# A one-core decoder block: q and k projected token-major and turned by transposing DMAs, instead of projected channel-major and scaled by a broadcast

## The chip, the cores and the metric

The kernel runs on one core of one Trainium2 chip. The metric is the device time of one execution in microseconds (us), lower is better. The kernel before takes 1475.8 us (median of three runs, 1473.98 to 1477.23).

## What is computed

A decoder block on `x` of 16 batches x 256 tokens x 512 channels: an attention with quantised weights and activations, then a mixing stage (a long convolution per head group), then a gated feed-forward. Only the first part is touched by the change:

```python
def _L0_attn_ref(x, w_qkv, w_proj):        # x: layer-normed, (16, 256, 512)
    def _bitlinear(x, w):                  # activations rounded per token, weights to {-1, 0, 1}
        xq, wq = act_quant(x), weight_quant(w)
        return jnp.einsum('bnc,oc->bno', xq, wq)
    qkv = _bitlinear(x, w_qkv).reshape(B, N, 3, H, D)      # 16 heads of 32 channels
    q, k, v = qkv[:, :, 0], qkv[:, :, 1], qkv[:, :, 2]
    attn = jnp.einsum('bnhd,bmhd->bhnm', q, k) * SCALE
    attn = softmax(where(causal, attn, NEG))
    out = jnp.einsum('bhnm,bmhd->bnhd', attn, v).reshape(B, N, C)
    return _bitlinear(out, w_proj)
```

`act_quant` rounds each token's 512 values to integers in steps of c, a number per token (its largest magnitude / 127). The kernel multiplies the integers and multiplies the products by c afterwards.

## The kernel before

Five engine programs are written out by hand with semaphores between them; each engine runs its own list in order (PE the matmuls, DVE, ACT, POOL the element-wise work, SP the DMAs). The attention part is a software pipeline over steps t. A step serves one **pair** of heads; a batch has 8 pairs, so a batch takes 8 steps, and what a batch needs once (norm, projections, finishing) hangs on fixed steps of those eight. Work of about four batches is in flight: batch b+4 is normed and projected while the scores of a later pair and the finishing of batch b run.

In each step, in the order of each engine's list:
- PE: `weigh` (probabilities x v, L686/L687), `row_max` (scores for the row maxima into `s_qk`, L629 to L634), `probabilities` (scores again, transposed, into `s_kq`, L659 to L669), then the once-per-batch work: `project_out` (L702), `multiply_v` (L616), `turn_xq` (L596), `spread_c` (L587), `turn_max` (L640), `turn_oq` (L694), `multiply_qk` (L607). `row_max` of a pair waits for DVE's `take_max` of the pair before it.
- ACT: `weighed` (L1502), `exponentials` (pT, L1488), `high_part` (pH, L1494), finishing of a batch (L1511 is its step size, of one output row), `high_qk` (L1474), norm and rounding, copies.
- DVE: `take_max` (blockmax, L1014), `scale_qk` (L994), v's halves (L1004, L1007), norm statistics, finishing (o_sb L1059, L1065, L1068, x_sb L1077).
- POOL: `low_part` (pL, L1846), `low_qk` (L1839), sums and pieces of feed-forward weights.
- SP: per batch one `x_scratch` store, 16 `pack` DMAs (L2057), one load of x, one store and one load of a weight piece.

Where q and k come from, for one batch (four parts of 128 x 512 each, one PSUM bank each, over four steps):
1. `multiply_qk` writes a bank **channel-major** (channels on partitions, tokens along the free axis), 8 matmuls of 256 columns.
2. The token's scale c then varies along the free axis, so it must be a row on all partitions: ACT writes it on a diagonal (`diagonal`, L1428), PE multiplies it by ones (`spread_c`, L587), ACT copies that to `cbc` (`copy_c`, L1435).
3. DVE multiplies the bank by `cbc` into `qkt`, f32 (`scale_qk`, L994); this frees the bank.
4. ACT copies `qkt` to f16, the high half (`high_qk`, L1474); POOL subtracts, the low half (`low_qk`, L1839; for batch 0 two of the four on DVE, L984).
5. SP regroups high and low halves with 16 DMAs into `pack` (`pack_qk`), which `row_max` and `probabilities` read.

The three PSUM banks of `misc1` go round among all once-per-batch users; a user waits for the release of the use three before.

These lines place the work (project step k of batch b is t = 8b - 13 + k):

```python
# PE: k = 0..3 multiply_qk(b, k)
# DVE:  if 1 <= k < 5: scale_qk(b, k - 1)
# ACT:  if 2 <= k < 6: high_qk(b, k - 2)        (after exponentials, high_part, finish)
# POOL: if 3 <= k < 7: low_qk(b, k - 3)
# SP:   if k == 7: pack_qk(b)
```

Batches 0 and 1 are prepared ahead of the steps.

## Time and profile before

| | |
|---|---|
| median of three runs | 1475.8 us (1473.98 to 1477.23) |
| the profiled execution | 1472.95 us, of which the span is 1471.2 us |
| mean granted PE clock | 0.99 of full speed |
| busy, share of the span | PE 95%, DVE 85%, POOL 79%, ACT 59% |
| attention part | about 26 to 470 us of the span |
| mixing and feed-forward | from about 470 us to the end; the change does not touch them |

Busy time says how long an engine had something in it; a matmul's bar is longer than the time it holds the engine, since matmuls are pipelined. The same holds in small for ACT and DVE: the bars of neighbours overlap by some 0.1 us, so what an instruction costs its engine is the distance from its start to the next one's start. A waiting engine is told by what ended its wait; the chain of waits follows the work that ended last backwards.

### The profile page before, as it was taken

The page shows a single profiled execution, that of the slowest core. Times are in us where ns is not written, and L with a number is a line of the kernel's source. Part 1 is how long each engine was busy: PE and PEld are TensorE (multiplying, and loading weights), DVE is VectorE, ACT ScalarE, POOL GpSimd, SP SyncE. Part 2 cuts the span into 40 slices and gives each one's busy share as a digit, 9 for nine tenths or more (in the row PEclk, how much of TensorE's full clock was granted, in tenths as well). Part 3 has the DMA queues.
Part 4 walks back from the last instruction along what each step waited for, and adds up shares of the span by engine and source line. Part 5 has one row for each costly group of instructions (what it writes and reads, how often), then busy time and mean ns, then how long its engine had stood idle before and what let it go on. Part 6 is the DMA issues. An engine that isn't in the chain of part 4 may idle for free.

```text
span 1471.2 us, 24208 instructions
## 1 busy us (share of the span) xinstructions
PE 1391.6 (95%) x8529; PEld 776.5 (53%) x8529; DVE 1243.6 (85%) x1987; ACT 870.4 (59%) x1434; POOL 1165.6 (79%) x893
## 2 busy tenths in 40 slices
PE   3788999999987997999999999999999999999998
PEld 2577878888765443344444444444444444444443
DVE  6889999999988897998888898899899889888521
ACT  5689999999876223555454545455465456544341
POOL 3389999999982878988887888878877887888432
PEclk9899999999999999999999999999999999999999
DMA  5554656565523533223423422432333333240001
GB/s 193 147 130 122 167 142 164 144 158 137 142 70 99 175 84 79 65 53 62 101 44 72 101 51 51 93 76 47 79 68 76 65 72 64 63 97 15 23 15 29
DMA packets 171588, 133.59 MB, mean 91 GB/s; under 512 B 120500, under 2 KB 124748, under 8 KB 171468
## 3 DMA queue, kind: packets, MB, share of 16 engines
q1 hardware_dynamic: 171276, 131.91, 36.5%
q8 instruction: 68, 1.11, 0.3%
q14 instruction: 52, 0.43, 0.1%
q10 hardware_dynamic: 192, 0.14, 0.1%
HBM read 50.67 MB, written 19.92 MB: 48 GB/s over the span
## 4 chain that ended last, share of the span: by engine, by line
PE 64%; DVE 13%; POOL 8%; issue 7%; ACT 6%; DMA 1%; SPq 0%; POOLq 0%; DVEq 0%; ACTq 0%
PE gu L868 20%; PE gu L882 11%; PE shared_bank L813 9%; PE y L837 3%; PE y L832 3%; PE y L829 3%; PE y L835 3%; PE y L838 3%; POOL pL L1846 2%; DVE blockmax L1014 2%; DVE o_sb L1059 2%; DVE z L1277 1%; DVE qkt L994 1%; PE misc L702 1%; ACT pH L1494 1%
## 5 line engine op out<-in xcount | busy, mean ns | idle before, releaser
L1718 ACT ACTIVATE shared<-shared_bank 128x512 f32<-128x512 f32 x162 | 96.2, 594 | 319.5 <-PE shared_bank L813 319.5
L1274 DVE TENSOR_TENSOR y<-shared,y 128x512 f32<-128x512 f32 x324 | 224.1, 692 | 42.1 <-ACT shared L1718 22.9
L1846 POOL TENSOR_TENSOR pL<-pT,pH 128x768 f16<-128x768 f32 x119 | 200.6, 1687 | 14.0 <-ACT pH L1494 7.8
L1281 DVE TENSOR_REDUCE oT<-z 128x64 f32<-128x512 f32 x256 | 175.6, 686 | 8.7
L868 PE MATMUL gu<-fT,wg 128*128 128x512 f16 x768 | 181.4, 379 | 1.5 <-DMA fT<-fnl 1.5
L868 PE MATMUL gu<-fT,wu 128*128 128x512 f16 x768 | 181.4, 379 | 0.0
L1277 DVE TENSOR_TENSOR z<-y,cT 128x512 f32<-128x512 f32 x236 | 162.4, 688 | 10.3 <-PE y L827 4.1
L1982 POOL TENSOR_TENSOR fuL<-fu,fuH 128x512 f16<-128x512 f32 x96 | 111.5, 1162 | 71.0 <-ACT fuH L1733 70.9
L882 PE MATMUL gu<-wd,fuH 128*128 128x512 f16 x384 | 145.5, 379 | 0.0
L882 PE MATMUL gu<-wd,fuL 128*128 128x512 f16 x384 | 145.5, 379 | 0.0
L1918 POOL TENSOR_TENSOR kv<-vT,cT 128x1024 f32<-128x1024 f32 x70 | 137.9, 1971 | 3.1 <-ACT vT L1673 3.1
L868 PEld LDWEIGHTS gu<-fT,wg 128*128 128x128 f16 x768 | 75.1, 98 | 121.0 <-issue 47.9
L868 PEld LDWEIGHTS gu<-fT,wu 128*128 128x128 f16 x768 | 75.1, 98 | 118.2 <-issue 45.7
L1488 ACT ACTIVATE pT<-s_kq,ws 128x768 f32<-128x768 f32 x124 | 111.4, 898 | 25.4 <-PE s_kq L669 19.9
L1014 DVE TENSOR_REDUCE blockmax<-s_qk 128x6 f32<-128x768 f32 x124 | 117.5, 948 | 3.9 <-PE s_qk L634 2.7
L813 PE MATMUL shared_bank<-kv_sum,toep 128*128 128x512 f32 x216 | 110.5, 593 | 0.3 <-POOL kv_sum L1906 0.3
L1906 POOL TENSOR_TENSOR kv_sum<-kv 128x1024 f32<-128x1024 f32 x27 | 63.7, 2360 | 55.0 <-DVE kv L1249 55.0
L1839 POOL TENSOR_TENSOR qkhl<-qkt,qkhl 128x512 f16<-128x512 f32 x62 | 83.9, 1355 | 20.7 <-ACT qkhl L1474 20.7
L1296 DVE SCALAR_TENSOR_TENSOR fu<-gu,cols,sil 128x512 f32<-128x512 f32 x96 | 71.3, 743 | 33.6 <-PE gu L868 33.6
L650 PE MATMUL s_kq<-pack 128*128 128x128 f16 x744 | 96.4, 220 | 0.0
L1494 ACT ACTIVATE pH<-pT 128x768 f16<-128x768 f32 x111 | 93.4, 841 | 0.0
L1249 DVE TENSOR_TENSOR kv<-vT,cT 128x1024 f32<-128x1024 f32 x58 | 74.0, 1276 | 14.2 <-ACT vT L1681 12.4
(251 smaller groups left out, 3589.9 us busy)
## 6 DMA issues: line engine op xcount, KB each, us to landing
pack<-qkhl SPq DMA_DIRECT2D x256, 128.0 KB, 2.6
x_sb<-in_x SPq DMA_DIRECT2D x16, 512.0 KB, 4.3
c_sb<-in_ctx SPq DMA_DIRECT2D x32, 256.0 KB, 4.1
hankel<-in_L_xattn_k SPq DMA_DIRECT2D x32, 256.0 KB, 4.1
out_y<-yo SPq DMA_DIRECT2D x32, 256.0 KB, 2.9
x_grp<-x_scratch SPq DMA_DIRECT2D x30, 256.0 KB, 3.6
x_scratch<-x_sb SPq DMA_DIRECT2D x14, 512.0 KB, 3.0
wraw<-in_L_attn_w_qkv SPq DMA_DIRECT2D x3, 1024.0 KB, 9.8
```

Of the source, the lines that this page charges most:

```text
L813: T.matmul(shared_bank[:], tap(h, (2, 0, 1)[part]), (kv_sum, kv12, kv_sum)[part][:, half * HB:(half + 1) * HB, :, :].rearrange("p b j i -> ...
L868: made = T.matmul(bank[:], (wg, wu)[which][:, cb, ib * P:(ib + 1) * P], fT[:, cb, part, :], start=cb == 0 and part == 0, stop=cb == CB - 1 ...
L882: made = T.matmul(bank[:], src[:, t * P:(t + 1) * P], wd[:, ib, :], start=ib == 0 and part == 0, stop=ib == IB - 1 and part == 1)
L1014: V.tensor_reduce(out=blockmax[b % 2][:, p, :], in_=score_tile(n)[:, 0:6, :], op=ALU.max, axis=AXIS.X, negate=True).then_inc(max_done, 1)
L1274: chain.step(V.tensor_tensor(bank[:], shared[2 * part + half][:], bank[:], op))
L1277: V.tensor_tensor(z[:], y, weight, ALU.mult).then_inc(m_zm, 1)
L1281: V.tensor_reduce(out=oT[h % 2][:, lb, own].rearrange("p (b j) -> p b j", b=HB), in_=z[:], op=ALU.add, axis=AXIS.X).then_inc(m_z, 1)
L1488: S.activation(pT[n % NP][:], scores_tile(n)[:, 0:6, :], ACT.Exp, scale=ws[:, 4:5]).then_inc(exp_done, 1)
L1494: S.activation(pH[n % NP][:], pT[n % NP][:], ACT.Copy).then_inc(high_act, 1)
L1846: G.tensor_tensor(pL[n % 2][:], pT[n % NP][:], pH[n % NP][:], ALU.subtract).then_inc(low_done, 1)
L1918: G.tensor_tensor(block(h, lb), vT[:, lb, :].rearrange("p (b i) -> p b i", b=B).unsqueeze(2).broadcast_to([P, B, M_POS, M_POS]), cT[h % 2] ...
L1982: G.tensor_tensor(fuL[ib][:], fu[n % 2][:], fuH[:, ib, :], ALU.subtract).then_inc(f_fl, 1)
```

## The change

q and k are projected **token-major** (tokens on partitions), as v already is. Then c is one number per partition, which ACT and DVE can apply while they read the bank: ACT writes the high half (bank x c, f16) straight from PSUM, DVE the low half (bank x c - high) straight from PSUM, both into a new tile `tok`. SP turns each part to channel-major with a transposing DMA (128 tokens x 1024 f16, high and low of one part) into `qkhl`, from where the 16 pack DMAs go on as before. The diagonal, its product with ones, `cbc`, `qkt`, DVE's `scale_qk` and POOL's `low_qk` are gone. ACT's `high_qk` stands one step earlier (k = 1..4) and ahead of `high_part`. A bank is now released by the low half.

(`low_qk` below is in DVE's program, `high_qk` in ACT's, `turn_qk` in SP's.)

```diff
-        qkt = [q(f"qkt{i}", [P, 2, N], F32) for i in range(3)]
+        tok = [q(f"tok{t}", [P, 2, 2, C], F16) for t in range(NT)]
...
-            def spread_c(b):
...
-            def multiply_qk(b, g2):
-                qk, g0 = qk_groups(g2)
-                bank = misc1.take(("qk", b, g2), w, (qk_scaled, 4 * b + g2 + 1))
+            def multiply_qk(b, s):
+                qk, t = token_tile(s)
+                bank = misc1.take(("qk", b, s), w, (qk_low, 4 * b + s + 1))
                 w.wait_ge(xqT_done, 2 * b + 2)
                 wT_ready(w, qk)
-                for g in range(2):
-                    o0 = qk * C + (g0 + g) * P
-                    for cb in range(CB):
-                        made = T.matmul(bank[:, g * N:(g + 1) * N], wqkvT[:, cb, o0:o0 + P], xqT[b % 3][:, cb, :],
-                                        start=cb == 0, stop=cb == CB - 1)
+                for cb in range(CB):
+                    made = T.matmul(bank[:], xqT[b % 3][:, cb, t * P:(t + 1) * P], wqkvT[:, cb, qk * C:(qk + 1) * C],
+                                    start=cb == 0, stop=cb == CB - 1)
...
+            def low_qk(b, s):
+                n, (qk, t) = 4 * b + s, token_tile(s)
+                w.wait_ge(qk_high, n + 1)
+                V.scalar_tensor_tensor(out=tok[t][:, qk, 1, :], in0=misc1.of["qk", b, s][:], scalar=small[b % 4][:, 12 + t:13 + t],
+                                       in1=tok[t][:, qk, 0, :], op0=ALU.mult, op1=ALU.subtract).then_inc(qk_low, 1)
...
                     if 1 <= k < 5:
-                        scale_qk(b, k - 1)
+                        low_qk(b, k - 1)
...
-            def diagonal(b):
...
-            def copy_c(b):
...
+            def high_qk(b, s):
+                n, (qk, t) = 4 * b + s, token_tile(s)
+                w.wait_ge(qk_pe, n + 1)
+                w.wait_ge(c_done, b + 1)
+                if b > 0:
+                    w.wait_ge(qk_turned, 64 * b)
+                S.activation(tok[t][:, qk, 0, :], misc1.of["qk", b, s][:], ACT.Copy, scale=small[b % 4][:, 12 + t:13 + t]).then_inc(qk_high, 1)
...
                 for i, blocks in turning(t - 1):
                     copy_weights(i, blocks)
+                for b, k in project_steps(t):
+                    if 1 <= k < 5:
+                        high_qk(b, k - 1)
                 if (n := pair(t, HIGH)) is not None and high_on_act(n):
                     high_part(n)
...
-                for b, k in project_steps(t):
-                    if 3 <= k < 7:
-                        low_qk(b, k - 3)
...
+            def turn_qk(b, s):
+                qk, t = token_tile(s)
+                w.wait_ge(qk_high, 4 * b + s + 1)
+                w.wait_ge(qk_low, 4 * b + s + 1)
+                if b >= 2:
+                    wait_packed(w, b - 2)
+                Y.dma_start(qkhl[b % 2][:, qk, :, :, t * P:(t + 1) * P].rearrange("p l g n -> p (l g) n"),
+                            tok[t][:, qk].rearrange("p l c -> p (l c)"), transpose=True).then_inc(qk_turned, 16)
...
                 for b, k in project_steps(t):
+                    if 2 <= k < 6:
+                        turn_qk(b, k - 2)
                     if k == 7:
                         pack_qk(b)
```

How the lists move, in the steady part. On **ACT**, in the two steps up to the finishing's step size (L1511 before, L1458 after; `tok` is written by `high_qk`). Before:

```order
L1474 ACTIVATE qkhl<-qkt 128x512
L1419 ACTIVATE xn<-xn,small 128x512
L1502 ACTIVATE oraw<-pv 128x2x130
L1488 ACTIVATE pT<-s_kq,ws 128x768
L1494 ACTIVATE pH<-pT 128x768
L1511 ACTIVATE osmall<-osmall 128x2
L1474 ACTIVATE qkhl<-qkt 128x512
L1428 ACTIVATE diag<-ident,small 128x128 x2
L1502 ACTIVATE oraw<-pv 128x2x130
```

After:

```order
L1421 ACTIVATE tok<-misc,small 128x512
L1441 ACTIVATE pH<-pT 128x768
L1381 ACTIVATE xn<-xn,small 128x512
L1449 ACTIVATE oraw<-pv 128x2x130
L1435 ACTIVATE pT<-s_kq,ws 128x768
L1441 ACTIVATE pH<-pT 128x768
L1458 ACTIVATE osmall<-osmall 128x2
L1449 ACTIVATE oraw<-pv 128x2x130
```

The last of a batch's four high halves stood behind the step size and now stands ahead of it, so all four are ahead of it where three were; the diagonal is gone.

On **SP**, one batch of the steady part. Before:

```order
L2066 DMA x_scratch<-x_sb 128x2x512
L2057 DMA pack<-qkhl 32x2x1024 x16
L2043 DMA x_sb<-in_x 128x2x512
L2082 DMA wq_scratch<-fw_out 128x768
L2077 DMA fw_raw<-in_L_ffn_gate_w 128x768
```

After:

```order
L1996 DMA x_scratch<-x_sb 128x2x512
L1987 DMA pack<-qkhl 32x2x1024 x16
L1975 DMA_TRANSPOSE qkhl<-tok 128x8x128
L1967 DMA x_sb<-in_x 128x2x512
L2012 DMA wq_scratch<-fw_out 128x768
L2007 DMA fw_raw<-in_L_ffn_gate_w 128x768
L1975 DMA_TRANSPOSE qkhl<-tok 128x8x128 x3
```

Four transposes per batch are added, one ahead of the load of x and three behind the weight piece.

## Rows read from the trace of the kernel before

**Rows 1.** Busy time in one batch period: us, then each engine's busy us (instructions).

```profile
219.26:244.08 24.82, 24.64 (x305) 20.20 (x304) 23.32 (x40) 24.29 (x49) 24.63 (x18) 1.00 0.58 152
```

**Rows 2.** Waits in 145 to 370 us: us in total, times, longest.

```profile
DVE small L944 <- ACT small L1403: 5.1, 9, 0.6
...
DVE osmall L1068 <- ACT osmall L1511: 1.8, 9, 0.2
```

**Rows 3.** Chain of waits, one period of it: start us, us, what.

```profile
223.66 0.65 PE misc L587 x4
...
226.35 0.90 ACT pT L1488
...
235.34 0.07 DVE small L944
...
251.16 0.90 ACT pT L1488
```

**Rows 4.** Timeline of ACT in that period: start us, us, instruction.

```profile
230.35 0.84 ACT L1494 ACTIVATE pH<-pT 128x768 f16<-128x768 f32 x1
...
234.08 0.61 ACT L1530 ACTIVATE oqT<-misc 128x512 bf16<-128x512 f32 x1
234.56 0.66 ACT L1474 ACTIVATE qkhl<-qkt 128x512 f16<-128x512 f32 x1
...
240.14 0.61 ACT L1474 ACTIVATE qkhl<-qkt 128x512 f16<-128x512 f32 x1
240.66 0.71 ACT L1419 ACTIVATE xn<-xn,small 128x512 f32<-128x512 f32 x1
241.27 0.36 ACT L1502 ACTIVATE oraw<-pv 128x260 f32<-128x260 f32 x1
```

**Rows 5.** Timeline of DVE in that period; idle time before stands in brackets.

```profile
230.41 0.68 DVE L994 TENSOR_TENSOR qkt<-misc,cbc 128x512 f32<-128x512 f32 x1
...
243.27 0.17 DVE L1068 RECIPROCAL osmall<-osmall 128x2 f32<-128x2 f32 x1 [0.19 <-ACT osmall L1511]
...
248.26 0.95 DVE L1014 TENSOR_REDUCE blockmax<-s_qk 128x6 f32<-128x768 f32 x1
```

**Rows 6.** Timeline of PE there.

```profile
249.53 0.38 PE L629 MATMUL s_qk<-pack 128*128 128x256 f16 x2
```

**Rows 7.** A group of POOL in 120 to 400 us: busy us, mean ns, idle before.

```profile
L1839 POOL TENSOR_TENSOR qkhl<-qkt,qkhl 128x512 f16<-128x512 f32 x46 | 64.1, 1394 | 0.0
```

**Rows 8.** A group of DVE in 120 to 400 us: busy us, mean ns, idle before.

```profile
L1007 DVE SCALAR_TENSOR_TENSOR vHL<-misc,small,vHL 128x512 f16<-128x512 f32 x23 | 17.3, 751 | 0.8
```

**Rows 9.** All instructions of line 1059: ns least/median/most, first and last start.

```profile
L1059 DVE TENSOR_TENSOR o_sb<-oraw,osmall x15: 1221/1524/2602, 111.6 to 451.7; 128x1024 f32<-128x1024 f32 x15
```

**Rows 10.** Transposing DMAs of the mixing part: SP's ns each, then us from issue to landing.

```profile
L2174 SPq DMA_TRANSPOSE c_sb<-planes x30: 1246/1267/1378, 491.0 to 1316.1; - x30
...
DMA to landing us min/median/max: 3.0/3.1/4.9
```

**Rows 11.** Timeline of SP over one batch: its first and last DMA of twenty.

```profile
246.93 0.38 SPq L2066 DMA_DIRECT2D x_scratch<-x_sb  x1
...
259.99 0.43 SPq L2077 DMA_DIRECT2D fw_raw<-in_L_ffn_up_w  x1
```

**Rows 12.** Timeline of batch 0, before the steps.

```profile
26.09 3.65 PE L607 MATMUL misc<-xqT,wqkvT 128*128 128x256 bf16 x32
...
32.09 10.55 SPq L2057 DMA_DIRECT2D pack<-qkhl  x16
...
44.70 0.38 PE L629 MATMUL s_qk<-pack 128*128 128x256 f16 x2 [1.87 <-DMA pack<-qkhl]
...
46.18 0.92 DVE L1014 TENSOR_REDUCE blockmax<-s_qk 128x6 f32<-128x768 f32 x1
```

**Rows 13.** Timeline of ACT in the first full batches.

```profile
100.47 0.90 ACT L1488 ACTIVATE pT<-s_kq,ws 128x768 f32<-128x768 f32 x1 [0.87 <-POOL pL L1846]
...
126.65 0.90 ACT L1488 ACTIVATE pT<-s_kq,ws 128x768 f32<-128x768 f32 x1
```

More of the change, by code:

```diff
@@ L140, in decoder_kernel @@
         xqT = [q(f"xqT{i}", [P, CB, N], BF16) for i in range(3)]
-        diag = q("diag", [P, NT, P], F32)
-        cbc = [q(f"cbc{i}", [P, N], F32) for i in range(2)]
         packs = [q(f"pack{i}", [P, 2, R, GQ, N], F16) for i in range(2)]
@@ L580, in weight_total @@
                 T.matmul(bank[:, 0:n], ones[:], wsums[:, first:first + n], start=True, stop=True).then_inc(wtot_pe, 1)
-            def spread_c(b):
-                bank = misc1.take(("cbc", b), w, (cbc_done, b + 1))
-                w.wait_ge(const_done, C_BASE)
-                w.wait_ge(diag_done, b + 1)
-                for t in range(NT):
-                    made = T.matmul(bank[:, t * P:(t + 1) * P], ones[:], diag[:, t, :], start=True, stop=True)
-                made.then_inc(cbc_pe, 1)
             def turn_xq(b, j):
@@ L1170, in vector_program @@
             for g2 in range(4):
-                scale_qk(0, g2)
-            for g2 in FIRST_LOW_ON_DVE:
-                low_first(g2)
+                low_qk(0, g2)
             max_in(1)
@@ L1419, in round_in @@
                 S.activation(xn[:, t, 0:C], xn[:, t, 0:C], ACT.Copy, bias=ROUND, scale=sm[:, 10 + t:11 + t]).then_inc(xround_done, 1)
-            def diagonal(b):
-                sm = small[b % 4]
-                w.wait_ge(c_done, b + 1)
-                w.wait_ge(const_done, C_BASE)
-                if b > 0:
-                    w.wait_ge(cbc_pe, b)
-                for t in range(NT):
-                    made = S.activation(diag[:, t, :], ident[:], ACT.Copy, scale=sm[:, 12 + t:13 + t])
-                made.then_inc(diag_done, 1)
-            def copy_c(b):
-                w.wait_ge(cbc_pe, b + 1)
-                if b >= 2:
-                    w.wait_ge(qk_scaled, 4 * (b - 1))
-                S.activation(cbc[b % 2][:], misc1.of["cbc", b][:, 0:N], ACT.Copy).then_inc(cbc_done, 1)
             def copy_xqT(b, j):
@@ L1578, in scalar_program @@
             round_weights(0)
-            diagonal(0)
             sign_weights(0)
@@ L1593, in scalar_program @@
                 round_in(1, i)
-            diagonal(1)
             moments(2)
@@ L1626, in scalar_program @@
                             round_in(b, i)
-                    if k == LOAD_AHEAD + 8:
-                        diagonal(b)
                     for j in range(2):
@@ L1868, in gpsimd_program @@
             power_in(1)
-            for g2 in range(4):
-                if g2 not in FIRST_LOW_ON_DVE:
-                    low_qk(0, g2)
             for t in STEPS:
@@ L2104, in sync_program @@
             Y.dma_start(wraw[3][:], w_proj.rearrange("(g t p) c -> g p t c", p=P, t=WB)[0]).then_inc(wraw_in[3], 16)
+            for s in range(4):
+                turn_qk(0, s)
             pack_qk(0)
```

68 lines of the change are left out of this document (9 added, 59 removed).

## The prediction

> **What bounds the kernel now.** I looked first at the busy time of one batch period of the attention part. A period is 24.82 us, and POOL is busy for 24.63 of it, PE 24.64, ACT 24.29, DVE 23.32 [rows 1]. So the shares do not name a bound: four engines are full, and the one that the change relieves most (POOL) looks like the fullest. Two other views are needed. The chain of waits, read over one period, says which loop of waits closes without slack, and the list of waits says which engine waits for which each time round.
>
> The chain does not pass through POOL in the steady part. From the exponential at 226.35 it runs down ACT's list to a small scale, over to DVE at 235.34, down DVE's list, then to PE, and back to ACT's exponential at 251.16 [rows 3]. That is eight steps later, 24.81 us, so this is a loop (**loop A**) that sets the period. Its PE leg holds the spreading of c, 0.65 us [rows 3]. The waits show the hand-overs, nine times in nine batches: DVE waits for ACT's L1403, and, in another place, for ACT's L1511 [rows 2]. The second is a loop of its own (**loop B**): down ACT's list from 226.35 to L1511, which releases DVE at 243.27 [rows 5], 16.92 us; down DVE's list to the blockmax that ends at 248.26 + 0.95 = 249.21 [rows 5], 5.94 us; 0.05 us until PE's `row_max`, which in fact starts at 249.53 [rows 6]; and 251.16 - 249.53 = 1.63 us to the exponential. Sum 24.54, so it has 0.27 us of slack now. Everything in it is order on one engine or a semaphore that the change keeps, so after the change the period cannot be shorter than loop B's new sum.
>
> **What the change does to ACT.** The high half costs 0.52 us of ACT now (240.14 to 240.66 [rows 4]). After, it reads PSUM and takes its scale from a tile. A copy of the same size out of PSUM without such a scale costs 0.48 (234.08 to 234.56 [rows 4]); a copy SBUF to SBUF with one costs 0.61 against the 0.52 without (240.66 to 241.27 [rows 4]), so the scale adds 0.09. I take 0.48 + 0.10 = 0.58, with bounds 0.48 and 0.61. The diagonal and the copy of `cbc` fall away, but ACT does them after L1511 and before 226.35: they lie in neither loop. What lies in them is high halves. They move one step forward. In loop A's ACT leg there is one now and there will be two: 2 x 0.58 - 0.52 = +0.64. In loop B's leg there are three now and all four after: 4 x 0.58 - 3 x 0.52 = +0.76.
>
> **DVE.** Four scalings at 0.68 us [rows 5] become four subtractions of the kind of L1007 at 0.75 [rows 8], +0.07 each, two of them in loop A, none in loop B's DVE leg. A new wait comes with them: DVE's first low half waits for ACT's high half of the same step. ACT would begin it where it now begins pH, 230.35 [rows 4], and end near 231.0; DVE now starts the scaling at 230.41 [rows 5]. DVE's list behind it is late by 0.6 us, `take_max` in it, for which PE's `row_max` waits. As a loop of its own: ACT from 226.35 to 231.0, 4.65; DVE's list from 230.41 to 249.21, 18.80, less its two waits for ACT (5.1 / 9 = 0.57 and 0.19 [rows 2, 5]) and with four times 0.07 more, 18.32; PE 1.68. That is 24.65, below B, so I cost it at nothing; without B's cover it would still be no more than today's period.
>
> **PE.** The 32 matmuls of 256 columns per batch become 16 of 512, the same columns, and I cost that at nothing. The spreading of c leaves loop A, -0.65. In loop B it saves nothing, because there PE is late on DVE's side of the wait.
>
> **Sums.** Loop A: 24.81 + 0.64 + 0.14 - 0.65 = 24.94. Loop B: 24.54 + 0.76 = 25.30. The period goes from 24.81 to 25.30, **+0.49 us**. With the bounds of the high half it is 24.90 or 25.42, so +0.1 to +0.6. L1511 stands behind four high halves in twelve periods (finishing of batches 0 to 11 beside projection of 4 to 15). The first of these is the early stretch below; the other eleven give 11 x 0.49 = **+5.4**.
>
> **POOL.** Its 64 subtractions (62 of them at L1839, mean 1394 ns [rows 7]) go, 5.6 us per batch. In the steady part nobody waits for them. In the first full batches somebody does: ACT's exponential at 100.47 had waited 0.87 us for POOL, and the eight steps to the one at 126.65 took 26.18 us [rows 13]. There loop B is lighter by the two copies of the finished rows (0.48 each [rows 4]), which no batch has yet: 25.30 - 0.96 = 24.34. That saves 1.8, with the wait ahead of it 0.9: **-2.7**, bounds 0 and -4.
>
> **SP and the DMAs.** Four transposes per batch at 1.27 us of SP each, 3.1 us from issue to landing [rows 10]. The twenty DMAs of a batch fill SP from 246.93 to 260.42 [rows 11], 13.5 us; with 5.1 more SP is busy 18.6 of 25. The first transpose comes behind the 16 packs and the others ahead of the store that now waits for x; the last can go once the fourth low half is there, about 243, and lands near 246. Pack starts after that store, at 247.3, as now. The packs land by 261.4 and the scores need them near 269, so 8 us cover this. In **batch 0** nothing covers it. The four parts leave PE 0.9 us apart from 26.09 [rows 12]: part one at 27.0, high half to 27.7, low half to 28.6, then four transposes issued 1.27 apart, the last at about 32.4, landed at 35.5. Pack starts at 32.09 now [rows 12], so it is 3.4 late, and so is the first `row_max`, which waits for the packs (1.87 us at 44.70 [rows 12]). DVE takes that maximum at 46.18, 0.9 later than it could; the delay that DVE's list passes on is about **+2.5**, bounds 1 and 5.
>
> **Total:** 2.5 - 2.7 + 5.4 = +5.2 on the profiled execution, 1472.95, gives 1478.2. The median of the runs, 1475.8, lies 2.85 above that execution, so on it 1481.0. The forecast's own range is 1475 to 1484: 4.4 less to 1.3 more from the high half, some 2 either way from the first batches. A measurement of this kernel can tell about 0.2% (3 us) from no change.
>
> **Rivals.** *1: POOL is the bound, and the kernel gets faster.* For it: POOL is busy 24.63 of 24.82 us [rows 1], and the early stretch shows it as the bound. Against it: in steady state the chain avoids it and nobody waits for it. If loop B is misread (if its hand-overs have slack that a different order opens), PE is next, and it loses the 0.65 of the spreading: 11 x -0.65 = -7.2, with -2.7 and +2.5 it is -7.4, so 1468.4. It decides if the period can reach 24.82 - 0.65 = 24.17: if the high halves in front of L1511 cost 0.3 us each, or if loop B shrinks elsewhere by 1.1. DVE could shrink: o_sb takes 1.22 us at best and 1.52 in the middle, 2.60 at most [rows 9], and the long ones fall together with POOL's work. With 1.22, loop A would be 24.63; loop B's DVE leg does not hold that instruction and stays. The Trainium skill (SBUF — State Buffer, "Who interferes with whom") says that a DVE instruction with two SBUF inputs and a GpSimd instruction that reads SBUF exclude each other for a whole instruction. By that rule the change frees DVE four times a batch, which speaks for this rival; the spread of o_sb agrees with it.
>
> *2: no change that can be told.* The high half costs 0.48 as the plain PSUM copy does; the period is 24.90, so 11 x 0.09 = +1.0 with -2.7 and +2.5 it is +0.8: 1476.6. The same comes if PE or DVE make up part of B.
>
> *3: the transposes become the bound.* SP is full when a transpose holds it for (25.3 - 13.5) / 4 = 2.95 us; alone they take at most 1.38 [rows 10], but none of those stood next to 16 packs. At 3.5 us a batch would take 27.5: +2.2 x 12 = +26, so 1507. That halving the number of q and k matmuls does nothing is part of the forecast, not a rival.
>
> **Chances.** Forecast 0.52, rival 1 0.20, rival 2 0.22, rival 3 0.06. Faster by over 0.2%: rival 1 and the low edge of 2, 0.22. Within 0.2%: most of rival 2 and the low edge of the forecast, 0.25. Slower: the rest, 0.53. The range reaches to rival 1's 1468 and 7 us over the forecast, 1467 to 1488; it leaves out rival 3 and the tails of rival 1.
>
> **What would show it.** Right: the steady period from exponential to exponential is about 25.3; DVE waits for the step size (L1458 after) 0.3 us or more each time; POOL idles 5 us a batch and nobody waits for it; the new high half costs 0.58 from start to start; the first `row_max` stands near 48. Wrong: a period of 24.2 with PE never waiting (rival 1); PE's `row_max` waiting for packs in steady state, or SP without pause (rival 3); DVE waiting long for high halves in each step would mean that ACT is late on PE's qk, which I cost at nothing.

## The result, and the profile after

The changed kernel takes **1481.3 us** (median of 5 runs, 1481.06 to 1482.41); the kernel before took 1473.98 us in the same session (5 runs, 1472.97 to 1477.23). The ratio is **1.0054**, 95% interval 1.0042 to 1.0066: slower, by more than the 0.2% that can be told. Run again later beside other kernels it gave 1.0057 (1.0041 to 1.0074). In one later session two executions, one of each kernel, took about two and two and a half times as long (2950.0 and 3762.11 us); they are left out of every median and ratio here. The forecast of 1481.0 us is met within 0.3, but partly by luck: the forecast difference (+5.2 us) was smaller than the measured one (0.54% of 1474, 8.0 us, interval 6 to 10), and the median that the forecast stood on, 1475.8 of three runs, was 1.8 us above that of the five here, of which those three are the first. On 1473.98 the same sum gives 1479.2. The profiled execution went from 1472.95 to 1481.3 us, +8.35, and that is what has to be accounted for.

I measure by one kind of mark, ACT's exponential of pair 2 of each batch (`pT`, L1435 after, L1488 before), as the prediction did:

| us | before | after | difference |
|---|---|---|---|
| first `row_max` | 44.70 | 49.23 | +4.53 |
| first exponential | 70.30 | 75.19 | +4.89 |
| pair 2, batch 0 to batch 2 | 50.82 | 49.77 | -1.05 |
| steady period, pair 2 to pair 2 | 24.81 | 25.24 | +0.43 |
| last exponential | 454.96 | 460.91 | +5.95 |
| from there to the end of the execution | 1017.99 | 1020.39 | +2.40 |

The steady part answers to [rows 1 to 4]. First the busy times in one period of the changed kernel, columns as in [rows 1]: span, PE, PEld, DVE, ACT, POOL, granted clock, DMA share, GB/s.

```profile
231.40:256.64 25.24, 24.81 (x285) 18.21 (x284) 23.68 (x40) 23.79 (x46) 18.78 (x14) 1.00 0.85 191
```

POOL fell from 24.63 to 18.78 us, as predicted, and the period got longer. ACT's busy time also fell, from 24.29 to 23.79, so once more the shares do not name the bound. The list of waits, 145 to 370 us (total, times, longest):

```profile
POOL pL L1776 <- ACT pH L1441: 37.0, 36, 1.6
POOL pL L1776 <- PE pv L665: 15.0, 9, 1.7
ACT pT L1435 <- PE s_kq L647: 13.1, 27, 0.8
...
DVE tok L958 <- ACT tok L1421: 5.1, 9, 0.6
...
DVE osmall L1032 <- ACT osmall L1458: 3.7, 9, 0.5
```

The wait of DVE for ACT's input step size, first in [rows 2], is gone. The other one, for the finishing step size (L1458, L1511 before), grew from 1.8 to 3.7 us over nine batches, 0.41 us each. The first low half waits 0.57 us each time for its high half, which is new. POOL stands in this list only as the one that waits, most of all for ACT.

The chain of waits of the changed kernel, one period (start, us, what):

```profile
231.40 0.90 ACT pT L1435
...
235.40 0.11 ACT tok L1421
...
247.39 0.78 ACT pT L1435
248.28 0.53 issue
248.81 0.20 ACT osmall L1458
249.11 0.70 DVE stats L902
...
253.99 0.96 DVE blockmax L978
255.00 0.39 PE s_qk L607 x2
...
256.64 0.90 ACT pT L1435
```

This is loop B and no longer loop A [rows 3]: ACT's list from 231.40 without a pause to L1458, then DVE to the blockmax of 253.99, PE, and the exponential 25.24 us after the first one. (The blockmax is DVE's maximum over the scores, for which PE's next scores wait.) ACT's timeline shows what filled the leg:

```profile
235.40 0.69 ACT L1421 ACTIVATE tok<-misc,small 128x512 f16<-128x512 f32 x1
235.97 0.85 ACT L1441 ACTIVATE pH<-pT 128x768 f16<-128x768 f32 x1
...
245.11 0.66 ACT L1421 ACTIVATE tok<-misc,small 128x512 f16<-128x512 f32 x1
245.68 0.83 ACT L1441 ACTIVATE pH<-pT 128x768 f16<-128x768 f32 x1
```

From start to start a high half takes 0.57 us (235.40 to 235.97, 245.11 to 245.68); four of them lie before L1458 (the other two at 238.96 and 241.88). The forecast was 0.58 and four. DVE goes on at 249.03, so ACT's leg is 17.63 us, against a forecast of 16.92 + 0.76 = 17.68.

Batch 0, from the timelines of PE and SP (start, us, instruction, idle before), answers to [rows 12]:

```profile
25.46 5.79 PE L585 MATMUL misc<-wqkvT,xqT 128*128 128x512 bf16 x16 [0.95 <-ACT wqkvT L1413]
...
49.23 0.38 PE L607 MATMUL s_qk<-pack 128*128 128x256 f16 x2 [4.11 <-DMA pack<-qkhl]
```

```profile
28.93 5.69 SPq L1975 DMA_TRANSPOSE qkhl<-tok  x4
36.62 10.42 SPq L1987 DMA_DIRECT2D pack<-qkhl  x16
```

The packs begin 4.53 us later than before (36.62 against 32.09), and the first `row_max` is late by exactly that. The 16 projection matmuls take 5.79 us; the same columns in 32 matmuls took 3.65 [rows 12]. The four transposes hold SP for 5.69 us, and 7.7 us lie between the start of the first and that of the first pack.

### The profile page after: what moved, and what is told of

Read it like the earlier page. It is cut to its first block, busy times and chain, and to the rows that moved or that the text cites. A ratio compares the mean times of both kernels' runs of the same rounds, so it can differ in the third digit from the quotient of the medians.

```text
span 1479.5 us, 23490 instructions
## 1 busy us (share of the span) xinstructions
PE 1392.5 (94%) x8209; PEld 743.1 (50%) x8209; DVE 1245.9 (84%) x1985; ACT 861.0 (58%) x1386; POOL 1079.7 (73%) x831
## 3 DMA queue, kind: packets, MB, share of 16 engines
q8 instruction: 66, 1.08, 0.3%
## 4 chain that ended last, share of the span: by engine, by line
PE 58%; ACT 13%; DVE 12%; issue 7%; POOL 5%; DMA 2%; SPq 1%; POOLq 0%; DVEq 0%; ACTq 0%
PE gu L842 19%; PE gu L856 11%; PE shared_bank L787 8%; ACT pT L1435 3%; ACT pH L1441 3%; PE y L803 3%; PE y L811 3%; PE y L806 3%; PE y L812 3%; PE y L809 3%; DVE blockmax L978 2%; DVE z L1239 2%; ACT oraw L1449 1%; DVE stats L902 1%; DMA v_sb<-planes 1%
## 5 line engine op out<-in xcount | busy, mean ns | idle before, releaser
L1435 ACT ACTIVATE pT<-s_kq,ws 128x768 f32<-128x768 f32 x124 | 111.6, 900 | 34.3 <-PE s_kq L647 33.8
L1672 ACT ACTIVATE fuH<-fu 128x512 f16<-128x512 f32 x96 | 59.7, 621 | 38.4 <-DVE fu L1258 38.4
```

The costliest lines, as they stand in the source:

```text
L1435: S.activation(pT[n % NP][:], scores_tile(n)[:, 0:6, :], ACT.Exp, scale=ws[:, 4:5]).then_inc(exp_done, 1)
```

## The experiments

Twelve runs of kernels, in four sessions, each beside the kernel before on the same chip. "Period" is the steady one from pair 2 to pair 2; "early" is the stretch from batch 0 to batch 2. These and the other columns behind the ratio come from one profiled execution each, so their differences from batch 0 and the mixing part hold scatter: after and after_again are the same kernel.

| kernel | us, median (runs) | ratio to before (95%) | first exp. | early | period | after the last exp. |
|---|---|---|---|---|---|---|
| before (profiled) | | 1 | 70.30 | 50.82 | 24.81 | 1017.99 |
| after (profiled) | 1481.3 (5) | 1.0054 (1.0042-1.0066) | 75.19 | 49.77 | 25.24 | 1020.39 |
| after_again | 1481.87 (5) | 1.0057 (1.0041-1.0074) | 76.66 | 49.76 | 25.23 | 1020.93 |
| step_on_dve | 1479.07 (5) | 1.0048 (1.0035-1.006) | 75.74 | 49.03 | 24.94 | 1020.43 |
| before_step_on_dve | 1474.01 (11) | 1.0012 (1.0003-1.0021) | 70.20 | 51.67 | 24.89 | 1018.64 |
| warm_first | 1481.36 (5) | 1.0062 (1.005-1.0075) | 75.81 | 52.65 | 25.23 | 1020.62 |
| plain_copies | 1479.44 (5) | 1.005 (1.0037-1.0063) | 75.53 | 49.77 | 25.23 | 1020.45 |
| both_steps_on_dve | 1489.38 (5) | 1.0116 (1.0097-1.0134) | 74.77 | 50.06 | 26.06 | 1018.29 |
| before_both_steps_on_dve | 1477.45 (10) | 1.0028 (1.0017-1.0039) | 72.54 | 51.32 | 24.89 | 1021.96 |
| before_no_low_halves | 1468.63 (9) | 0.997 (0.9958-0.9981) | 69.73 | 47.77 | 24.79 | 1019.32 |
| max_before_low | 1477.12 (7) | 1.0028 (1.0018-1.0039) | 73.58 | 48.54 | 24.94 | 1019.73 |
| max_before_low_alone | 1479.04 (5) | 1.0045 (1.0031-1.0058) | 74.85 | 49.23 | 25.23 | 1020.78 |
| single_column_steps | 1480.7 (5) | 1.0059 (1.0047-1.0072) | 75.22 | 49.28 | 25.22 | 1020.23 |
| two_highs_on_pool | 1496.85 (5) | 1.0163 (1.0146-1.018) | 73.80 | 48.48 | 26.79 | 1021.46 |

### Is it loop B? The hand-over taken out

```diff
 # VectorE, finish(b, 3)
+w.wait_ge(omax_done, b + 1)
+V.tensor_scalar(step, am, 1.0 / 127.0, None, ALU.mult).then_inc(ostep_done, 1)
 w.wait_ge(ostep_done, b + 1)
 V.reciprocal(inv, step).then_inc(oscale_done, 1)
 # ScalarE, finish(b, 3)
-w.wait_ge(omax_done, b + 1)
-S.activation(step, am, ACT.Copy, scale=1.0 / 127.0).then_inc(ostep_done, 1)
```

> The changed kernel, with the finishing's step size (largest magnitude / 127) computed by DVE itself in place of ACT's L1458, so that DVE no longer waits there for ACT. Theory (loop B, through four high halves on ACT and that hand-over, sets the period of 25.24 us): the next loop is A, 24.94 by the prediction's sum, so the steady period falls by about 0.3 us and the kernel gains 2.5 to 4 us on the changed one. Rival (PE's wait for score maxima, the transposes, or DVE's wait for the high half of the first part set the period): period still 25.2, gain under 1 us.

> The same edit in the kernel before. Theory: there loop B had 0.27 us of slack and loop A set the period, so no gain: period 24.8, time within 0.1% of the kernel before. Rival (the hand-over costs the same wherever it stands): it gains there too, 2 to 4 us.

In the changed kernel the period fell from 25.24 to 24.94, the 0.3 that was expected, so the edge from L1458 to DVE did set it. The expected gain in time, 2.5 to 4 us, can't be told from the runs: the ratio is 1.0048 against 1.0054, with intervals that overlap. In the traces it is there: from pair 2 of batch 0 to pair 2 of the last batch this kernel takes 366.35 us, the changed one 369.16, 2.8 less. The same edit made in the kernel before gained nothing there (24.89 against 24.81, and 0.12% slower), which is right if another loop was the longer one in it. The fall ends at 24.94, the figure computed for loop A, but the chain of this kernel does not pass through the input step size. It runs over the first high half, the prediction's third loop, which was put at 24.65:

```profile
230.34 0.90 ACT L1439 ACTIVATE pT<-s_kq,ws 128x768 f32<-128x768 f32 x1
...
235.06 0.75 DVE L958 SCALAR_TENSOR_TENSOR tok<-misc,small,tok 128x512 f16<-128x512 f32 x1 [0.57 <-ACT tok L1425]
...
252.64 0.95 DVE L978 TENSOR_REDUCE blockmax<-s_qk 128x6 f32<-128x768 f32 x1
...
253.65 0.39 PE L607 MATMUL s_qk<-pack 128*128 128x256 f16 x2
```

These are timelines of ACT, DVE and PE. The legs are 235.06 - 230.34 = 4.72, then 253.59 - 235.06 = 18.53 of DVE's list (the blockmax ends at 252.64 + 0.95 = 253.59), then 255.29 - 253.59 = 1.70 to the next exponential: 24.95. The prediction had 4.65, 18.32 and 1.68. DVE's leg is the one that was mostly too short, by 0.21, and the reason can be read off two instructions of the changed kernel, against one of the kernel before (the other is in [rows 9]; all instances of a line: ns least/median/most):

```profile
L1017 DVE TENSOR_TENSOR oraw<-oraw x9: 1298/1317/1321, 163.5 to 365.3; 128x512 f32<-128x512 f32 x9
```

```profile
L1023 DVE TENSOR_TENSOR o_sb<-oraw,osmall x15: 1209/1220/2596, 115.9 to 457.6; 128x1024 f32<-128x1024 f32 x15
```

```profile
L1053 DVE TENSOR_TENSOR oraw<-oraw x9: 747/764/770, 159.0 to 357.4; 128x512 f32<-128x512 f32 x9
```

`o_sb` lost 0.30 us (1.52 to 1.22), as the rule cited under rival 1 would have it. But with POOL's subtractions gone, POOL's other work has moved against DVE's list, and the sum of the first halves of `oraw` now takes 1.31 instead of 0.76. Together +0.25, about what DVE's leg was short of. Timelines of POOL and DVE, first of the kernel before, then of the changed one, show how:

```profile
231.98 1.64 POOL L1846 TENSOR_TENSOR pL<-pT,pH 128x768 f16<-128x768 f32 x1
...
233.40 0.77 DVE L1053 TENSOR_TENSOR oraw<-oraw 128x512 f32<-128x512 f32 x1
```

```profile
238.87 1.08 POOL L1783 TENSOR_TENSOR oraw<-oraw 128x512 f32<-128x512 f32 x1
...
239.18 1.32 DVE L1017 TENSOR_TENSOR oraw<-oraw 128x512 f32<-128x512 f32 x1
```

Both sums end 0.55 us after the POOL instruction in which they began: 234.17 - 233.62, and 240.50 - 239.95. That holds for all 24 of these sums between 100 and 400 us in the two kernels (0.54 to 0.56), and `o_sb` always ends 1.07 to 1.10 us after one. So what such an instruction cost DVE here was its own time and what was left of POOL's instruction when it began.

### Do the transposes cost anything in the steady part?

```diff
-tok[t][:, qk].rearrange("p l c -> p (l c)"), transpose=True)
+tok[t][:, qk].rearrange("p l (g n) -> p (l g) n", n=P))
```

> The changed kernel, with each transposing DMA replaced by a plain DMA of the same bytes between the same tiles (q and k stay token-major in qkhl, so that the scores are of other numbers). Theory (transposes cost only in batches 0 and 1, where nothing covers SP and the landing): steady period unchanged at 25.2, SP per batch 2.5 us less, first row_max about 2.5 us earlier (four issues 0.6 us apart in place of 1.3, landing 0.4 sooner), gain 2 to 3 us. Rival (transposes next to packs slow the steady part): the period falls to 24.9 or less, gain over 5 us.

A transposing DMA holds SP for 1.30 us (median of 48), a plain one for 0.62, and the median time to landing is 4.5 us for both. The period is 25.23 either way, so rival 3 is out. The first `row_max`, expected about 2.5 us earlier, is at 49.04, 0.2 earlier, and the gain of 2 to 3 us did not come (ratio 1.0050). From the start of the first copy to that of the first pack 7.4 us pass (28.82 to 36.24), against 7.7 with transposes. What costs in batch 0 is one more stage of DMAs, not that it turns. (In this kernel q and k are not turned and the scores are meaningless; the work after them is the same.)

### Does the pace of batch 0's matmuls cost what it seems to?

```diff
 turn_weights(0)
+keep_busy(s_qk[:, 0, :], 16)
 for g2 in range(4):
     multiply_qk(0, g2)
```

> The changed kernel, with 16 matmuls of 128 columns on idle data put between batch 0's weight transposes and its q and k projections, where PE is idle for 1.0 us and where the kernel before had the spreading of c. Theory: the 16 projection matmuls of 512 columns ran at 634 ns where they take 379 in steady state, because PE fell to its lower level over that pause; with PE kept busy they run at 379, the first row_max comes 1.5 to 2 us earlier than 49.23, and the kernel gains 1.5 to 2 us. Rival (they are slow for another reason, such as the bank waiting for ACT and DVE): no gain.

```profile
25.67 3.41 PE L585 MATMUL misc<-wqkvT,xqT 128*128 128x512 bf16 x15 [0.48 <-ACT wqkvT L1414]
...
48.10 0.58 PE L607 MATMUL s_qk<-pack 128*128 128x256 f16 x2 [5.36 <-DMA pack<-qkhl]
```

The timeline of PE shows the projection at full pace again: 3.41 us for the columns that took 5.79 (one of the 16 matmuls has no record). The packs then began at 35.47 and the first `row_max` stood at 48.10, 1.1 us earlier instead of 2.4; its own matmuls, behind 5.36 us of waiting, now ran at a granted clock of 0.50, the lower of its two levels (48.10 to 50.00 us; in the changed kernel it was 0.89 from 49.20 to 50.70), and the first exponential is at 75.81, no earlier. The edit buys nothing. Several other kernels had the fast projection by themselves (3.63 us in step_on_dve and max_before_low), and their first exponentials, 75.74 and 73.58, show that it hardly counts. In the long early stretch of this execution, 52.65, DVE waited 2.50 us for a weight piece and then took 2.11 us for the instruction that reads it (1.00 in the changed kernel). Both kernels wait there (1.74 before, 1.85 after).

### The other hand-over, and a wait that was not on my list

```diff
 # VectorE, scale_in(b); taken from ScalarE
+V.tensor_scalar(sm[:, 12:14], sm[:, 8:10], 1.0 / 127.0, None, ALU.mult).then_inc(c_done, 1)
 w.wait_ge(c_done, b + 1)
 V.reciprocal(sm[:, 10:12], sm[:, 12:14]).then_inc(inv_done, 1)
```

> The changed kernel with both step sizes (the finishing step size at L1458 and the input's at L1365) computed by VectorE, each beside the reciprocal that follows it, so that neither hands over to ScalarE and back. Theory of the loops: the steady period is the longest loop of hand-overs. With the finishing step on VectorE alone it was 24.94, which is the loop over the input's step size (loop A). With both gone what is left is the loop over the wait for the first high half (24.65), VectorE's own work and PE's (about 23.5 to 24): steady period 24.3 to 24.65, 0.3 to 0.6 less than 24.94 over 9 to 12 batches, so 3 to 7 us under step_on_dve: 1472 to 1476 us, level with before. Rival, ScalarE's order is what is slow (any high half between the exponentials and their high parts costs its 0.58, whatever waits on it): the period stays at 24.9 to 25.2, time 1478 to 1481.

> The kernel before with the same two step sizes on VectorE. Theory: in before GpSimd is busy 24.6 of 24.8 us in a period and is the next bound right behind the loop, so taking both hand-overs out gains nothing: period 24.7 to 24.9, time 1472 to 1475. The relief of GpSimd that the change brings would then be worth something only once the hand-overs are gone too. Rival, GpSimd's instructions start early enough and its busy time holds idle inside it: the period falls to 24.3 to 24.6, time 1467 to 1470.

Both theories missed on the first: the period rose to 26.06, and the time to 1489.4 us. In the kernel before it stayed at 24.89, with POOL busy 24.82 of it, as expected; the median came out 2.5 us above the expected band. Timelines of DVE and of POOL in both_steps_on_dve show where the time went:

```profile
244.22 1.08 DVE L918 TENSOR_SCALAR small<-small 128x2 f32<-128x2 f32 x1
...
252.81 0.15 DVE L1036 TENSOR_SCALAR osmall<-osmall 128x2 f32<-128x2 f32 x1
```

```profile
243.63 1.65 POOL L1776 TENSOR_TENSOR pL<-pT,pH 128x768 f16<-128x768 f32 x1 [0.54 <-ACT pH L1446]
```

Two numbers per partition took 1.08 us (the other instances of L918 beyond 100 us: 1.07 to 1.54). L918 began at 244.22 inside POOL's `pL` and ended at 245.30, 0.02 us behind it (243.63 + 1.65 = 245.28). The same operation at L1036 began when POOL's `pL` of 250.41 was over, and took 0.15. This is no single case: in both_steps_on_dve, its twin of the kernel before and two_highs_on_pool, 44 of these instructions between 100 and 400 us began while a POOL instruction ran, and all 44 ended 0.02 to 0.04 us after it, whether that made them 0.17 or 1.54 us long. The loop over the first high half contains L918: 24.94 + 1.08 = 26.02, measured 26.06. The Trainium skill (SBUF — State Buffer, "Who interferes with whom") says that `tensor_scalar` can take the pair of ports that DVE and GpSimd share, and that the one that comes second is then blocked for the whole instruction; VectorE: DVE Perf Modes ("What auto-detection actually checks") wants for it, besides one source and a destination in SBUF, that the outermost dimensions longer than one are even or equal. A single column has no such dimension; I took it that it then stays clear of the pair. That was tried, for both step sizes (the input's is shown):

```diff
-V.tensor_scalar(sm[:, 12:14], sm[:, 8:10], 1.0 / 127.0, None, ALU.mult).then_inc(c_done, 1)
+V.tensor_scalar(sm[:, 12:13], sm[:, 8:9], 1.0 / 127.0, None, ALU.mult)
+V.tensor_scalar(sm[:, 13:14], sm[:, 9:10], 1.0 / 127.0, None, ALU.mult).then_inc(c_done, 1)
```

> both_steps_on_dve (1489.4 us, period 26.06) with each step size computed by two instructions of one column instead of one of two columns. Theory: there L918, 2 numbers per partition, took 1.07 us and more each time because it had to wait out a GpSimd instruction (it ended with the pL beside it), while the same instruction at L1036, where GpSimd was idle, took 0.15; a single column does not take the way that they share. Then each takes 0.15 us (0.08 apart), the loop over the first high half and VectorE's list is 24.94 + 0.2 = 25.1 to 25.2, and the time 1480 to 1482. Rival, the instruction waits for something else on its own engine (the maximum just before it is still in the pipe): the pair takes 1.1 us or more, and period and time stay at 26.0 and 1489.

```profile
L918 DVE TENSOR_SCALAR small<-small x11: 136/136/141, 115.0 to 366.6; 128x1 f32<-128x1 f32 x11
```

All eleven took 0.14 us, and each of them ran inside one of POOL's `pL`, which it did not wait out; the period is 25.22 and the time 1480.7 us, as expected (25.1 to 25.2 and 1480 to 1482), against 26.06 and 1489.4 for the two-column form (ratios 1.0059 and 1.0116). The trace agrees with the rule. Two instructions in place of one are here worth 0.84 us a batch.

### What is GpSimd's relief worth by itself?

```diff
+few = 2 if b > 1 else N
-G.tensor_tensor(hl[:, qk, 1, g0:g0 + 2, :], qkt[n % 3][:], hl[:, qk, 0, g0:g0 + 2, :],
+G.tensor_tensor(hl[:, qk, 1, g0:g0 + 2, 0:few], qkt[n % 3][:, :, 0:few], hl[:, qk, 0, g0:g0 + 2, 0:few],
```

> The kernel before with GpSimd's subtraction for the low halves of q and k cut to 2 columns from batch 2 on (the low halves are left out there): the relief of GpSimd alone, without any other part of the change. Theory: the steady period is set by the loop over the input's step size and stays at 24.8; only the early stretch, where GpSimd also has the weights' work, gains, 1 to 2.7 us (the changed kernel's was 1.05): time 1470 to 1473. Rival, GpSimd is the bound (the prediction's first rival): the period falls to about 24.3 or less, over 12 batches 5 to 7 us, time 1465 to 1468.

```profile
222.20:246.99 24.79, 24.61 (x305) 20.21 (x304) 23.28 (x40) 24.26 (x48) 21.07 (x18) 1.00 0.58 153
```

POOL fell to 21.07 us per period, and the period is 24.79, unchanged: rival 1 is out where it was aimed, in the steady part. The early stretch fell by 3.05 us, to 47.77, a little more than the prediction's -2.7, and the next period by another 0.5 (25.29 to 24.80). The ratio is 0.997 (0.9958 to 0.9981), the time 1.4 us under the theory's band. So the relief is worth some 4 us, nearly all of it before the steady part; in the changed kernel 1.05 of the 3.05 is left.

### Filling the wait of the first low half

```diff
 for b, k in project_steps(t):
+    if k == 1:
+        for bm, km in batches(t, NORM_AT, LOAD_AHEAD + 11, 2):
+            if km == LOAD_AHEAD + 4:
+                max_in(bm)
     if 1 <= k < 5:
         low_qk(b, k - 1)
```

> step_on_dve (finishing step on VectorE) with one more change in VectorE's order: in the step in which it meets both, it takes the maximum of the next batch's input (L913, 1.2 us) before the first low half (L958), so that the 0.57 us that it waits for the first high half are filled. Theory: the loop that gave step_on_dve its 24.94 is the prediction's third one (first high half on ScalarE, then VectorE's list to a blockmax, PE, exponential), which the prediction put at 24.65. With the wait filled it is 24.94 - 0.57 = 24.37, and the period falls to whatever comes next, 24.4 to 24.7; over 10 to 12 batches 3 to 6 us under step_on_dve, 1473 to 1476: level with before. Rival, loop A (over the input's step size on ScalarE, computed as 24.94) gave it: the maximum starts 0.6 us earlier at most, the period stays at 24.8 to 24.95 and the time at 1478 to 1479.

> The changed kernel with only the reordering on VectorE (maximum of the input before the first low half), the finishing step size left on ScalarE. Theory: its period of 25.24 is loop B (ScalarE's list with four high halves to L1458, then VectorE), in which the first low half does not lie: no gain, period 25.2 to 25.25, time as the changed kernel's, ratio to before about 1.005. Rival: the same wait of VectorE is what costs in the changed kernel too; then the period falls to about 24.9 and the time by 3 us or more.

Alone, the new order changed nothing in the steady part, 25.23: loop B does not hold that wait. On top of step_on_dve the period stayed at 24.94, where the theory had it fall to 24.4 to 24.7; the rival gave the period, and the time came out 1 us under the rival's. The list of waits of max_before_low says what took over:

```profile
DVE small L920 <- ACT small L1376: 5.1, 9, 0.6
```

DVE's wait for the first high half, 0.57 us each, is gone from the list, and a wait for the input's step size has come in its place, the same 0.57. That is loop A. The timelines of DVE and PE close it, from the exponential at 227.71 to the one at 252.65:

```profile
237.34 0.17 DVE L920 RECIPROCAL small<-small 128x2 f32<-128x2 f32 x1 [0.56 <-ACT small L1376]
...
250.00 0.95 DVE L980 TENSOR_REDUCE blockmax<-s_qk 128x6 f32<-128x768 f32 x1
```

```profile
251.01 0.39 PE L607 MATMUL s_qk<-pack 128*128 128x256 f16 x2
```

ACT's leg to L920 is 237.34 - 227.71 = 9.63, DVE's list without a pause to 250.95 is 13.61, and 1.70 follows to the exponential: 24.94, the figure that the prediction computed for loop A. The two loops were level, and shortening one showed the other. A further path is level with them: the chain of this kernel goes down ACT's list to 243.46, through PE's `pv` and scores to 249.95, and back to ACT, so that a gain in loop A alone would not have shown either. The early stretch fell to 48.54 and the time to 1477.1 us, the best of the changed kernels and still 0.28% over the kernel before.

### Using the room on GpSimd

Batch pairs 1 and 5: the `f16` copy of the probabilities is made by GpSimd, right ahead of its own low part.

```diff
 # GpSimd, low_part(n)
+if high_on_pool(n):        # n % 8 in (1, 5), batches 3 to 14
+    w.wait_ge(exp_done, n + 1)
+    w.wait_ge(pv_pe, n - NP + 1)
+    G.tensor_copy(pH[n % NP][:], pT[n % NP][:]).then_inc(high_pool, 1)
```

> max_before_low (finishing step on VectorE, input maximum before the first low half; 1477.1 us, period 24.94, GpSimd busy some 19 us of it) with the high parts of two of a batch's eight pairs (pairs 1 and 5, batches 3 to 14) moved from ScalarE to GpSimd, which has 5 to 6 us to spare in a period since the change and is idle 1.5 us ahead of pair 5's low part while it waits for just this high part. Theory: all loops that were measured at 24.9 to 25.2 start down ScalarE's list from the same exponential; its work is what the change overfilled. Pair 1's high part (0.73 us from start to start) lies in all of them, pair 5's only in loop B and in the stretch from ScalarE over PE. Loop A falls to 24.94 - 0.73 = 24.2; the period to 24.2 to 24.5, where PE's own work comes next (busy 24.3 to 24.8 now, with waits in it). Over 11 periods 5 to 8 us under max_before_low: 1469 to 1472, level with or under before. Rivals: GpSimd's copies take over 2 us each, or VectorE's instructions with two inputs in SBUF wait for them, and the period stays at 24.9 or rises (1477 or more); or PE is the bound at 24.8 already, and the time stays above 1475.

```profile
241.75 1.52 POOL L1799 TENSOR_TENSOR oraw<-oraw 128x512 f32<-128x512 f32 x1
...
247.40 0.82 POOL L1788 CAST pH<-pT 128x768 f16<-128x768 f32 x1
...
250.88 1.64 POOL L1792 TENSOR_TENSOR pL<-pT,pH 128x768 f16<-128x768 f32 x1 [0.95 <-ACT pH L1458]
```

```profile
240.52 1.82 DVE L1025 TENSOR_TENSOR oraw<-oraw 128x512 f32<-128x512 f32 x1
...
243.93 2.02 DVE L1031 TENSOR_TENSOR o_sb<-oraw,osmall 128x1024 f32<-128x1024 f32 x1
...
251.27 1.28 DVE L1042 TENSOR_SCALAR osmall<-osmall 128x2 f32<-128x2 f32 x1
```

A clear miss: 26.79 instead of 24.2 to 24.5. The copy itself is cheap (0.82 us), but the chain of this kernel now runs through POOL: its L1788, L1792 and L1799 into DVE's L1031. DVE shows no idle time in front of `o_sb`, so the tight place is likely just ahead: its `oraw` sum ends at 242.34, again 0.55 us after a POOL instruction (a `pL` that ends at 241.79), and POOL's list ahead of that holds the first of the new copies. On DVE three instructions then meet POOL's: the `oraw` sum 1.82 (1.31 in the changed kernel), `o_sb` 2.02 (1.22) and the step size 1.28 (0.16 in step_on_dve), which again ends with POOL's `pL` (252.55 and 252.52). The theory of this run had these waits as its rival, and the rival came true. That is 0.51 + 0.80 + 1.12 = 2.43 us of DVE's list; 24.94 + 2.43 = 27.4 is more than enough for the rise of 1.85. How the rise divides between POOL's longer list and DVE's longer instructions was not separated.

## Why the prediction was right, and where it was not

The mechanism was right: loop B took over in the steady part and POOL's relief counted only before it. That the forecast time lies 0.3 us from the measured median is luck: of the terms one was 2.4 too small, one 1.65 too large a gain, one 1.3 too large a loss, and the median that they were added to was 1.8 too high.

**Right, and shown by runs.**

- *The bound.* Not POOL: with its work cut by 3.5 us a period the kernel before keeps its 24.79 (before_no_low_halves). Loop A before, loop B after: the list of waits, the chain, and the two kernels that took B's hand-over out (25.24 to 24.94 in the changed one, nothing in the one before).
- *Loop B.* 16.92 + 0.76 of ACT was forecast, and the sum 25.30. Measured: four high halves at 0.57, period 25.24, so +0.43 where +0.49 was said.
- *Loop A after the change,* 24.94: the legs of max_before_low add up to it (9.63 + 13.61 + 1.70), and so does its period. ACT's leg grew by the forecast 0.64 (8.99 to 9.63). The rest is not the path of the forecast: that went over PE's list and took off the spreading of c there, while this one goes down DVE's list to the blockmax, which was 13.68 before without its wait for ACT and is 13.61 now. That the sums agree to 0.01 is partly luck.
- *The wait for L1458.* At least 0.3 us each was forecast; 3.7 / 9 = 0.41.
- *SP and the transposes in the steady part,* costed at nothing: plain_copies has the same period, though the transposes land in 4.5 us (median) rather than the 3.1 assumed.
- *POOL early.* -2.7 for relief alone; before_no_low_halves has -3.05.

**Mis-sized.**

- *Batch 0, +2.5 with bounds 1 and 5: it is +4.9 at the first exponential.* Two steps of it were off. The pack start was put 3.4 us late and was 4.53 late; the 2.1 us by which 16 matmuls of 512 columns ran longer than the 32 had been costed at nothing, and warm_first gave back half of that when they were fast. And the step from the pack start to the total took off 0.9 for slack in DVE's list, which did not show: the delay arrives in full, and 0.36 more. The figure scatters: after_again, the same kernel, has its first `row_max` at 49.12 and the first exponential at 76.66, +6.4. PE's mean granted clock from that `row_max` to 60 us was 0.69 there and 0.84 in the profiled changed kernel, a cost that the prediction had no term for.
- *The early stretch, -2.7: it is -1.05.* The term for POOL was right by itself. I had put the period from batch 1 to batch 2 at 24.34, loop B without the two copies, and it took 25.96, where before_no_low_halves, with the kernel before's ACT list, took 24.28. step_on_dve brings it down to 25.21, so the hand-over L1458 was in it. What the sum left out altogether is a weight piece that DVE waits for, with which the chain of this stretch begins in the changed kernel. Its reader on DVE, in the kernel before and in the changed one:

```profile
99.50 1.29 DVE L1137 TENSOR_SCALAR fw_pow<-fw_raw 128x768 int32<-128x768 int32 x1 [1.74 <-DMA fw_raw<-in_L_ffn_gate_w]
```

```profile
105.11 1.00 DVE L1101 TENSOR_SCALAR fw_pow<-fw_raw 128x768 int32<-128x768 int32 x1 [1.85 <-DMA fw_raw<-in_L_ffn_gate_w]
```

  Before, that wait ends 0.97 us ahead of the exponential of 100.47 that opens this period; after, 0.58 us behind the one of 104.53, inside the period. before_no_low_halves has no such wait and 24.28; max_before_low has one of 0.47 and 24.42. How the 1.6 us divide between the piece and loop B was not separated.
- *The steady sum, +5.4 over eleven periods: they give +4.1* (126.65 to 398.38 before, 130.49 to 406.30 after). Eight of them show the full +0.43; the first is 0.08 shorter than before, because POOL's load still made it 25.29 there, and the last two are longer by 0.22 and 0.52. Only eight of the eleven ran at the steady period.
- *A late period of the kernel before,* which no term stood for: the one from 398.38 took 24.68 and was 2.0 us longer than the same one of before_no_low_halves (22.71) and of the changed kernel (22.72). PE's clock made most of that. The same matmuls, from a `row_max` to the weighing behind it, in the kernel before and in before_no_low_halves (columns as in [rows 1], the granted clock behind POOL):

```profile
411.26:415.42 4.16, 4.16 (x28) 2.74 (x29) 2.48 (x3) 1.21 (x3) 2.18 (x2) 0.59 0.00 0
```

```profile
406.74:409.24 2.50, 2.50 (x28) 1.84 (x29) 2.47 (x3) 0.86 (x2) 2.18 (x2) 1.00 0.00 0
```

  That is 1.66 of the 2.0 us. In both PE had stood idle for 1.38 us just before; in one execution the clock then fell to its lower level (0.50 from 411.60 to 414.60) and in the other it did not.
- *The third loop, 24.65 and costed at nothing.* It is 24.94, level with loop A: the `oraw` sum took 0.55 more, `o_sb` 0.30 less. Loop B covered it, so it cost the forecast nothing; it is why step_on_dve and the reordering gave less than hoped.
- *The rest of the execution,* costed at nothing, is 2.40 us longer. The last column of the table speaks for scatter: single executions of kernels that are identical there lie between 1017.99 and 1021.96, the four that are or derive from the kernel before span that whole range by themselves, and the kernel before's happened to be the lowest. A real difference of up to about 1 us (means 1020.3 for the ten changed kernels, 1019.5 for the four others) is not excluded.

In sum: 4.9 - 1.05 + 4.1 - 2.0 (the odd period of before) + 2.4 (mostly scatter) = 8.35. The forecast's three terms made 5.2; two of them erred in the same direction by 4.0 together, the steady one by 1.3 the other way.

**The rivals.** Rival 1 fell in the steady part (before_no_low_halves: same period with POOL at 21.07) and stands in the early stretch, as the prediction had it. Rival 2 needed a high half of 0.48; it is 0.57. Rival 3 fell with plain_copies. That the kernel is not slower through DVE's new wait either is what max_before_low_alone speaks for: that wait is filled there and the period is the same, though DVE then waits the same 0.57 us for the input's step size (5.0 us in nine batches).

**Left open.** Why PE's clock fell in the odd period of the kernel before and not in the same place of the others. How much of the early stretch's 1.6 us is the weight piece. How much of two_highs_on_pool's loss is each of its two causes. And no kernel tried that computes the reference beats the kernel before: that would need the ACT list lightened ahead of L1458 and of the input step size at once, without a new instruction in POOL's list ahead of its `oraw` sum.

## What to carry to other kernels

When four engines are full, sum each loop of hand-overs by itself, before and after the change, and write down those that are level with the longest: the gain of an edit ends at the next loop, and here three lay within 0.3 us of each other (25.24, 24.95, 24.94). Freeing an engine that nobody waits for is worth only what it is worth in the stretch where somebody does. And before a small instruction is moved to VectorE beside a busy GpSimd, look for its form: two columns took 1.08 us where one took 0.14.

## What the runs showed of the hardware that I had not expected

- A `tensor_scalar` of 128x2 `f32` in SBUF ended within 0.04 us of the end of the GpSimd instruction that was running when it began, 44 times of 44 in three kernels (0.17 to 1.54 us long); 0.15 with GpSimd idle; 0.136 as 128x1, eleven times in the midst of a GpSimd instruction.
- Moving GpSimd's work in time changes the duration of DVE's two-input instructions in both directions: the `oraw` sum 0.76 to 1.31 us and `o_sb` 1.52 to 1.22, for the same operands. Their end follows GpSimd's: 0.55 and 1.08 us after the end of the instruction that was running.
- The projection matmuls of batch 0 took 5.79 us for 16 x 512 columns in one execution, 5.21 in another of the same kernel, and 3.41 behind filler matmuls. 3.41 is some 0.21 us for 512 columns, the pace of 2.4 GHz (512 / 2.4 = 213 ns). The pause ahead of them does not decide it: it was 0.95 us in the slow cases, 0.48 behind the fillers, and 0.95 again in step_on_dve, where they took 3.63. The granted clock over the slow stretch reads 1.00 all the same:

```profile
25.46:31.25 5.79, 5.79 (x16) 2.02 (x16) 1.60 (x3) 2.09 (x4) 0.91 (x2) 1.00 0.19 36
```
